# Group sums of a normalisation moved from TensorE to VectorE's shuffles, and one weighted addition of the kernel mixing moved to ScalarE and a DMA

## The chip, the cores and the metric

One core of one Trainium2 chip. The metric is the device time of one execution in microseconds (us), lower is better. TensorE multiplies, VectorE (DVE) and ScalarE (ACT) compute on whole tiles of 128 partitions, GpSimd (POOL) computes little here and issues the accumulating DMAs, SyncE (SP) issues the plain ones.

## The reference

```
x: 16 images, 128 channels, 32 x 32, f32
gn(v): normalise over each group of 4 channels (32 groups), eps 1e-5
routing = sigmoid(mean(gn(x), pixels) @ w_route.T + b_route)   # 4 weights per image
y  = conv3x3(gn(x), w_experts)            # 4 experts, 128 -> 128 channels each
y  = sum over experts of routing[e] * y[e]
h  = x + silu(y * inv + shift)            # inv, shift from the batch-norm parameters
out = h + conv3x3(gn(h), sign(W))
```

The kernel mixes the four experts' weights with an image's routing first, and then does one convolution with the mixed kernel.

## The kernel before

Channels lie on the 128 partitions, so a group of the normalisation is four neighbouring partitions. All 16 images stay in SBUF (tile X, residual added in place). The five engines run five instruction streams that are written out by hand and tied with semaphores. The order of each stream is fixed.

**Image stages.** Image 0 is convolved directly in the head of the program (direct_part), while the weights arrive. Images 1 to 15 use a Winograd-like form along the rows: VectorE makes six points of each 4-row tile (all_rows, inner_rows, transform_minus, transform_plus, transform_ends, into V), TensorE multiplies each point with three taps (minus_points, plus_point, end_points, L562, f32), VectorE brings them back (inverse_sums, inverse_inner, inverse_outer, into y). ScalarE applies SiLU (L936), and POOL adds y to X by an accumulating DMA (residual, L450). That is h. The second convolution, with the sign weights, takes h in two f16 parts: hi and lo (ScalarE's L951 and L958, VectorE's low_part L1309), 18 products each (sign_half, L598).

**The loop.** Iteration t = 1 to 15 of each engine's stream works on several images at once. TensorE does the points of image t and then the sign convolution of image t - 1. VectorE does, in this order, the transforms of image t + 1, its mix with expert 1, the inverse of image t, pool_routes, the low part of image t - 1, the mixes with experts 2 and 3, and the kernel rows (even_rows, kernel_rows) of image t + 1. ScalarE's order in iteration t is quoted below with the statistics.

**The statistics.** The chain of number c normalises two things at once: x of image c (column IN) and h of image c - LAG (column MID), LAG = 3. In iteration t it is c = t + 2. ScalarE fills four columns of stats: the negated means and the sums of squared deviations of both. TensorE multiplies them with a matrix that sums over each group (group_stats, into PSUM tile ps). ScalarE makes variances of it (variances: gdev2, less, two ve), POOL the power -0.5 (power, L446), ScalarE the biases and, from them, hi and hn:

```
var_mid(t - 1); add_variance(c, MID); variances(c)
copy_minus(t); evacuate(t - 2); deviation(c); centring(c); pads(c)
bias(c, MID); split_hi(t - 1); pooled_plane(c); split_hn(t - 1)
silu(t); mean_mid(t); mean_in(c + 1); var_in(c + 1)
squares(c + 1); add_variance(c + 1, IN); routing(c); mix(c)
```

variances(c) waits for the group sums of the column that stands directly before it. In the trace its first instruction is the one that writes gdev (L848). split_hi(t - 1) is what TensorE waits for before its high-part products of iteration t.

**The mixing.** Tile U, three buffers in a ring, holds an image's mixed kernel, 128 x 1152. ScalarE writes route[0] * expert 0 (mix, L908), and VectorE adds the other three in place, one instruction each (mix(i, e), L1186).

**The head.** ScalarE makes the statistics of images 0, 1 and 2 between the four parts of image 0's first mix. The chains of images 1 and 2 go through TensorE (group_mean L510, group_var L521), between the products of image 0 (L552).

Of the kernel before, what the change touches and what calls it, by code (L numbers as in the profile page):

```python
# [10 lines left out]
ALU = mybir.AluOpType  # L11
# [45 lines left out]

RING = 3
QUARTERS = 4

# [7 lines left out]
def build(nc, x, w_experts, w_sign, params, out):  # L68
# [5 lines left out]
    with ExitStack() as ctx:  # L74
# [81 lines left out]
        zr = sb("zr", [C, B])  # L156
        centre = sb("centre", [C, B, 2])
        pooled = sb("pooled", [C, B, E])
        th = sb("th", [C, B, E])
        route = sb("route", [C, B, E])  # L160
# [43 lines left out]
        pooled_ready = sem("pooled_ready")  # L204
        logits_ready = sem("logits_ready")
        th_ready = sem("th_ready")
        route_ready = sem("route_ready")
# [74 lines left out]
        def mixes_before(t):  # L282

            return len(DIRECT_PARTS) * (E - 1) * min(t, ND) + (E - 1) * rank(t)

# [151 lines left out]
        def _(pool):  # L437
# [37 lines left out]
            for t in range(1, B + 1):  # L475
                power(t + LAG - 1)
                if 0 <= t - 2 < B - LATE:
                    add_output(t - 2)
                if ND <= t < B and t not in DVE_RESIDUAL:
                    residual(t)  # L480

        @block.tensor
        def _(pe):
# [38 lines left out]

            def group_stats(c):

                if c < B:
                    pe.wait_ge(nm_in_ready, c + 1)
                pe.wait_ge(nm_mid_ready, c - LAG + 1)
                pe.wait_ge(spread_ready, columns_to(c))
                wait_bank(c)
                step = 1 if c < B else 3  # L530
                mm_(gstats(c, 0, 4, step), gmat[:], stats[:, c, 0:4:step], start=True, stop=True).then_inc(gvar_ready, 1)  # L531

            def route_logits(i):
                pe.wait_ge(pooled_ready, i + 1)
                mm_(logits(i), ones[:], pooled[:, i, :], start=True, stop=True).then_inc(logits_ready, 1)  # L535

# [21 lines left out]

            def point(t, bank, j, k, weights):
                for n, kx in enumerate(KX_ORDER):  # L560
                    c0, c1 = reach(kx, 0, W, W)
                    mm = mm_(bank[:, :, j, c0:c1], tap_weights(weights, kx),  # L562
                             V[t % 2][:, :, k, c0 + kx - 1:c1 + kx - 1], start=(n == 0), stop=(n == K - 1))
                return mm
# [9 lines left out]

            def plus_point(t, j):
                r = rank(t)
                k = (P1, P2)[j]
                pe.wait_ge(v_ready, 5 * r + 4)
                wait(pe, sums_ready, 2 * r)
                pe.wait_ge(kernel_ready, 4 * r + k + 1)  # L580
                mm = point(t, pa, j, k, UM[t % 2][:, k, :])
                if j == 1:
                    mm.then_inc(m_ready, 1)

# [116 lines left out]
            for t in range(1, B + 1):  # L701
                c = t + LAG - 1
                if t < B:
                    minus_points(t)
                    if t > 1:
                        group_stats(c)
                        sign_half(t - 2, 1, 1, TAP_ORDER[-1:])
                    plus_point(t, 0)
                    if t == 1:
                        group_stats(c)  # L710
                    plus_point(t, 1)
                    end_points(t)
                if t == 1:
                    pe.wait_ge(ws_ready, 1)
                if t == B:
                    sign_conv_last()
                elif t == B - 1:
                    sign_half(t - 1, 0, 0)
                    sign_half(t - 1, 0, 1, TAP_ORDER[:5])
                    group_mean(c + 1)  # L720
                    sign_half(t - 1, 0, 1, TAP_ORDER[5:])
                    sign_half(t - 1, 1, 0, TAP_ORDER[:5])
                    last_residual()
                    group_var(c + 1)
                    sign_half(t - 1, 1, 0, TAP_ORDER[5:])
                    sign_half(t - 1, 1, 1)
                else:
                    sign_half(t - 1, 0, 0)
                    sign_half(t - 1, 0, 1)
                    if c < B:  # L730
                        route_logits(c)
                    sign_half(t - 1, 1, 0)
                    sign_half(t - 1, 1, 1, TAP_ORDER[:-1])

        @block.scalar
        def _(act):
# [87 lines left out]
            def deviation(c):  # L824

                if c < B:
                    act.wait_ge(nm_in_ready, c + 1)
                    activation(dev[:, c:c + 1], gnm(c, IN), ACT.Identity, bias=nm(c, IN), scale=-1.0) \
                        .then_inc(dev_ready, 1)
# [6 lines left out]
            def variance(c):  # L836

                k = cols(c)[0]
                last = c == CHAINS - 1
                act.wait_ge(gvar_ready, c + 1)  # L840
                activation(ve[:, c, k:k + 1], gvar(c, k), ACT.Identity, bias=epsilon[:, last:last + 1],
                           scale=1.0 / (HW * (LAST_SCALE if last else ACT_SCALE) ** 2)).then_inc(ve_ready, 1)

            def variances(c):

                a, b = cols(c)
                act.wait_ge(gvar_ready, c + 1)
                activation(gdev2[:, c, a:b], gstats(c, a, b), ACT.Square, bias=base[:, 0:1]).then_inc(gdev2_ready, 1)  # L848
                act.wait_ge(gdev2_ready, c - LAG + 1)
# [3 lines left out]
                for k in range(a, b):  # L853
                    op = activation(ve[:, c, k:k + 1], gvar(c, k), ACT.Identity, bias=less[:, c, k:k + 1],  # L854
                                    scale=1.0 / (HW * ACT_SCALE ** 2))
                op.then_inc(ve_ready, 1)

            def bias(c, k):
                act.wait_ge(rstd_ready, c + 1)
                activation(nbias[:, c, k:k + 1], gnm(c, k), ACT.Copy,  # L860
                           scale=rstd[:, c, k:k + 1]).then_inc((nbias_mid_ready, nbias_in_ready)[k], 1)
# [7 lines left out]
            def centring(i):  # L869

                if in_one(i):
                    act.wait_ge(gvar_ready, i + 1)
                else:
                    act.wait_ge(gnm_ready, gnm_chain(i))
                for n, factor in enumerate((1.0, P1_SUM)):
                    activation(centre[:, i, n:n + 1], gnm(i, IN), ACT.Copy, scale=-factor).then_inc(centre_ready, 1)

# [22 lines left out]
            def mix(i):  # L900
# [176 lines left out]
        def _(dve):  # L1077
# [77 lines left out]
            def top_rows():  # L1155
# [5 lines left out]
                 .then_inc(xn_top_ready, 1)  # L1161

            def pool_routes(c):
                if c < B:
# [285 lines left out]
            for t in range(1, B):  # L1450

                if t == B - 1:
                    sign_points()
                all_rows(t + 1)
                if t == 1:
                    residual(0)
                inner_rows(t + 1)
                transform_minus(t + 1)
                transform_plus(t + 1)
                transform_ends(t + 1)  # L1460
                mix(t + 1, 1)
                inverse_sums(t)
                inverse_inner(t)
# [39 lines left out]
```

## Time and profile before

| | |
|---|---|
| three runs | 273.08, 273.12, 273.42 us, median 273.12 |
| profiled execution | 273.27 us, of which 271.2 us lie between its first and last instruction |
| busy | TensorE 263.0, VectorE 255.0, ScalarE 213.5, POOL 45.2 us |
| granted TensorE clock | 0.999 of full speed, mean |
| DMA | 35.20 MB, 130 GB/s mean |

The profile shows one execution. "Busy" adds up the spans of instructions. The chain that ended last is followed back from the last instruction to what released each step. In a timeline a line gives start, duration, engine, source line, operation, tile written <- tiles read, the count, and in brackets the idle time of that engine before it with what ended it. Consecutive instructions of an engine may overlap by about 0.1 us.

### The profile page before, as it was taken

The numbers are of one execution on the slowest core, as the hardware profiler recorded it, in microseconds if no ns is written. First come the engines' busy times: TensorE is split into PE (matmuls) and PEld (weight loads), VectorE is DVE, ScalarE is ACT, GpSimd is POOL, SyncE is SP. The second block draws the span as 40 slices with busy tenths as digits, with TensorE's granted clock in tenths as the row PEclk, the third lists the DMA queues.
The fourth block names the chain that finished last, engine by engine and source line by source line (L and its number), as shares of the span: only waits on it lengthen the run. The fifth ranks groups of instructions, "written<-read, shape, count | busy, mean of one in ns | idle before, by whom it ended". The sixth has DMA issues, their size and how long they took to land.

```text
span 271.2 us, 4199 instructions
## 1 busy us (share of the span) xinstructions
PE 263.0 (97%) x1339; PEld 182.2 (67%) x1339; DVE 255.0 (94%) x461; ACT 213.5 (79%) x469; POOL 45.2 (17%) x61
## 2 busy tenths in 40 slices
PE   7889899999999999999999999999999999999993
PEld 7545766758485766859586675848576685858663
DVE  5789999999999999999999999999999999995985
ACT  2798898898979788898979799797979886735870
POOL 2011030313121021312112021211202021210110
PEclk9999999999999999999999999999999999999999
DMA  7998856452716455361825546271645536282407
GB/s 205 416 369 300 272 194 155 69 128 51 144 77 111 123 79 155 34 124 77 140 95 77 155 68 148 37 138 80 106 126 79 156 34 124 79 137 97 77 2 155
DMA packets 10245, 35.20 MB, mean 130 GB/s; under 512 B 1264, under 2 KB 1904, under 8 KB 10224
## 3 DMA queue, kind: packets, MB, share of 16 engines
q0 software_dynamic: 4176, 15.21, 33.2%
q1 hardware_dynamic: 5616, 19.34, 19.3%
q10 hardware_dynamic: 432, 0.39, 0.4%
q8 instruction: 11, 0.18, 0.3%
q14 instruction: 10, 0.08, 0.1%
HBM read 11.34 MB, written 16.25 MB: 102 GB/s over the span
## 4 chain that ended last, share of the span: by engine, by line
PE 92%; DMA 3%; DVE 1%; SPq 1%; issue 1%; ACT 0%; DVEq 0%; ACTq 0%
PE pc L598 42%; PE pa L562 14%; PE pe_ L562 14%; PE pb L562 14%; PE pd L552 4%; DMA we<-w_experts 3%; PE ps L531 1%; PE ps L535 1%; SPq L409 0%; PE pa L635 0%; PE pb L635 0%; DVE X L1402 0%; SPq L413 0%; PE pc L521 0%; DVE sums L1384 0%
## 5 line engine op out<-in xcount | busy, mean ns | idle before, releaser
L1186 DVE SCALAR_TENSOR_TENSOR U<-we,route,U 128x1152 f32<-128x1152 f32 x45 | 63.7, 1415 | 0.5
L598 PE MATMUL pc<-lo,ws 128*128 128x496 f16 (+3 forms) x270 | 62.0, 375 | 0.0
L598 PE MATMUL pc<-hi,ws 128*128 128x496 f16 (+3 forms) x270 | 59.8, 375 | 0.0
L598 PEld LDWEIGHTS pc<-hi,ws 128*128 128x128 f16 x270 | 26.4, 98 | 29.3
L598 PEld LDWEIGHTS pc<-lo,ws 128*128 128x128 f16 x270 | 27.7, 106 | 26.3
L446 POOL TENSOR_TENSOR rstd<-ve,nhalf 128x2 f32<-128x2 f32 (+1 forms) x19 | 17.4, 915 | 142.2 <-ACT ve L854 120.5
L562 PE MATMUL pa<-V,UM 128*128 128x256 f32 (+1 forms) x180 | 40.7, 375 | 0.0
L562 PE MATMUL pb<-V,UM 128*128 128x256 f32 (+1 forms) x180 | 40.5, 375 | 0.0
L562 PE MATMUL pe_<-V,U 128*128 128x256 f32 (+1 forms) x180 | 40.5, 375 | 0.0
L562 PEld LDWEIGHTS pb<-V,UM 128*128 128x128 f32 x180 | 34.2, 190 | 5.3 <-issue 0.4
L562 PEld LDWEIGHTS pe_<-V,U 128*128 128x128 f32 x180 | 34.2, 190 | 3.9
L562 PEld LDWEIGHTS pa<-V,UM 128*128 128x128 f32 x180 | 34.0, 190 | 3.5
L936 ACT ACTIVATE y<-y,bn_shift,bn_tiles 128x1024 f32<-128x1024 f32 x14 | 17.4, 1240 | 6.4 <-DVE y L1288 6.4
L450 POOL DMA_DIRECT2D X<-y x14 | 12.4, 882 | 56.6 <-ACT y L936 56.6
L762 ACT ACTIVATE junk_mid<-X,stats 128x1024 f32<-128x1024 f32 x15 | 17.1, 1139 | 5.8 <-DMA X<-y 5.5
L848 ACT ACTIVATE gdev<-ps,base 128x2 f32<-128x2 f32 (+1 forms) x15 | 3.9, 263 | 19.9 <-PE ps L531 19.8
L951 ACT ACTIVATE hi<-X,nbias,rstd 128x1024 f16<-128x1024 f32 (+2 forms) x16 | 18.9, 1187 | 0.5
L908 ACT ACTIVATE U<-we,route 128x1152 f32<-128x1152 f32 x15 | 18.8, 1256 | 0.5
L1309 DVE TENSOR_TENSOR lo<-hn,hi 128x1024 f16<-128x1024 f32 x15 | 18.3, 1219 | 0.4 <-ACT hn L958 0.4
L958 ACT ACTIVATE hn<-X,nbias,rstd 128x1024 f32<-128x1024 f32 x15 | 18.4, 1226 | 0.0
L1218 DVE SCALAR_TENSOR_TENSOR e_rows<-X 128x1024 f32<-128x1024 f32 x15 | 18.3, 1219 | 0.0
L748 ACT ACTIVATE junk_var<-X,stats 128x1024 f32<-128x1024 f32 x15 | 17.2, 1147 | 0.5
(168 smaller groups left out, 400.3 us busy)
## 6 DMA issues: line engine op xcount, KB each, us to landing
X<-x SPq DMA_DIRECT2D x15, 512.0 KB, 5.8
out<-X SPq DMA_DIRECT2D x15, 512.0 KB, 2.6
out<-ev POOLq DMA_DIRECT2D x15, 512.0 KB, 5.5
X<-y POOLq DMA_DIRECT2D x14, 512.0 KB, 4.5
we<-w_experts SPq DMA_DIRECT2D x2, 768.0 KB, 8.8
ws_raw<-w_sign SPq DMA_DIRECT2D x1, 576.0 KB, 11.4
we<-w_experts SPq DMA_DIRECT2D x1, 512.0 KB, 6.6
out<-X SPq DMA_DIRECT2D x1, 384.0 KB, 2.8
```

The lines of the kernel that those rows point to most:

```text
L446: g.tensor_tensor(rstd[:, c, a:b], ve[:, c, a:b], nhalf[:, a:b], ALU.pow).then_inc(rstd_ready, 1)
L562: mm = mm_(bank[:, :, j, c0:c1], tap_weights(weights, kx), V[t % 2][:, :, k, c0 + kx - 1:c1 + kx - 1], start=(n == 0), stop=(n == K - 1))
L598: mm = mm_(rows[:, r0 - first // W:r1 - first // W, c0:c1], ws[:, tap * C:(tap + 1) * C], plane((hi, lo)[part], i)[:, r0 + ky - 1:r1 + ky ...
L748: activation(junk["var"][:], img(i), ACT.Square, bias=nm(i, IN), accum_out=var[:, i, IN:IN + 1]).then_inc(var_in_ready, 1)
L762: activation(junk["mid"][:], img(i), ACT.Square, bias=nm(c, MID), accum_out=var[:, c, MID:MID + 1]).then_inc(var_mid_ready, 1)
L908: activation(nine(U[i % RING]), expert(0), ACT.Copy, scale=route[:, i, 0:1]).then_inc(mix_first, 1)
L936: activation(flat3(y[i % 2][:]), flat3(y[i % 2][:]), ACT.Silu, bias=bn_shift[:, 0:1], scale=bn_tiles[:, 0:1], accum_out=ysum[:, i:i + 1]). ...
L951: activation(plane(hi, i)[:, first:last, :], img(i).rearrange("p (h w) -> p h w", h=H)[:, first:last, :], ACT.Identity, bias=nbias[:, c, M ...
L958: activation(hn[:], img(i), ACT.Identity, bias=nbias[:, c, MID:MID + 1], scale=rstd[:, c, MID:MID + 1]).then_inc(hn_ready, 1)
L1186: v.scalar_tensor_tensor(out=nine(U[i % RING]), in0=expert(e), scalar=route[:, i, e:e + 1], in1=nine(U[i % RING]), op0=ALU.mult, op1=ALU.a ...
L1218: v.scalar_tensor_tensor(out=flat3(e_rows[:]), in0=flat(X[:, i, 0:H, :]), scalar=-4.0, in1=flat(X[:, i, 2:2 + H, :]), op0=ALU.mult, op1=AL ...
L1309: v.tensor_tensor(lo[i % 2][:, 0:HW], hn[:], hi[i % 2][:, 0:HW], ALU.subtract).then_inc(lo_ready, 1)
```

## The change

Three parts, with the order around them:

- **Head.** On ScalarE the deviations and the centring of image 1 stand before the fourth part of the first mix, and variance before pads for images 1 and 2.
- **Group sums.** From chain 3 on, TensorE's group_stats goes. VectorE has group_sums: two rounds of a stream_shuffle within 32 partitions (partition number with bit 1, then bit 2 flipped) and an addition, into gsum. ScalarE reads gsum, and divides by the group size in its scale. It gets one more small activation, middle_mean. group_sums stands behind inner_rows in iterations 2 to 14, behind mix(2, 1) in iteration 1, and first in iteration 15.
- **Mixing.** From image 3 on ScalarE also writes route[1] * expert 1 into a tile (scale_second), and POOL's queue adds this tile to U by an accumulating DMA (add_scaled), behind the residual. VectorE's mix with expert 1 goes for these images. The mixes with experts 2 and 3 stay behind the low part, and the first of them waits for the DMA.

```diff
@@ gpsimd
+            def add_scaled(i):
+                pool.wait_ge(mix_first, firsts_before(i) + 1)
+                pool.wait_ge(scaled_ready, i - SCALED_FROM + 1)
+                g.dma_start(flat(U[i % RING][:]), scaled[:], accum_op=ALU.add).then_inc(scaled_added, 16)
...
                     residual(t)
+                if t + LAG - 1 < B:
+                    add_scaled(t + LAG - 1)
@@ tensor
-            def group_stats(c):
...
-                mm_(gstats(c, 0, 4, step), gmat[:], stats[:, c, 0:4:step], start=True, stop=True).then_inc(gvar_ready, 1)
...
                     minus_points(t)
                     if t > 1:
-                        group_stats(c)
                         sign_half(t - 2, 1, 1, TAP_ORDER[-1:])
-                    plus_point(t, 0)
-                    if t == 1:
-                        group_stats(c)
-                    plus_point(t, 1)
+                    plus_points(t)
                     end_points(t)
@@ scalar
             def variances(c):
...
-                act.wait_ge(gvar_ready, c + 1)
-                activation(gdev2[:, c, a:b], gstats(c, a, b), ACT.Square, bias=base[:, 0:1]).then_inc(gdev2_ready, 1)
+                act.wait_ge(gsum_ready, c - LAG + 1)
+                activation(gdev2[:, c, a:b], gsum[:, c, a:b], ACT.Square, bias=base[:, 0:1],
+                           scale=1.0 / GSIZE).then_inc(gdev2_ready, 1)
...
+            def middle_mean(c):
+                activation(gmid[:, c:c + 1], gsum[:, c, MID:MID + 1], ACT.Copy, scale=1.0 / GSIZE) \
+                    .then_inc(gmid_ready, 1)
...
+            def scale_second(i):
+
+                wait(act, scaled_added, 16 * (i - SCALED_FROM))
+                activation(scaled[:].rearrange("p (g n) -> p g n", n=C), expert(1), ACT.Copy,
+                           scale=route[:, i, 1:2]).then_inc(scaled_ready, 1)
...
             var_in(1)
-            mix_first_part(0, 3)
             deviations(1)
             centring(1)
+            mix_first_part(0, 3)
+            variance(1)
             pads(1)
-            variance(1)
...
             centring(2)
+            variance(2)
             pads(2)
-            variance(2)
...
                 variances(c)
+                middle_mean(c)
...
                     mix(c)
+                    scale_second(c)
@@ vector
+            def group_sums(c):
+
+                a, step = 0, 1 if c < B else 3
+                data = stats[:, c, 0:4:step]
+                if c < B:
+                    dve.wait_ge(nm_in_ready, c + 1)
+                dve.wait_ge(nm_mid_ready, c - LAG + 1)
+                dve.wait_ge(spread_ready, columns_to(c))
+                for n, bit in enumerate((1, 2)):
+                    source = (data, pairs[:, 0:4:step])[n]
+                    target = (pairs[:, 0:4:step], gsum[:, c, 0:4:step])[n]
+                    wait(dve, pairs_ready, c - LAG + n)
+                    v.stream_shuffle(swapped[:, n, 0:4:step], source, [p ^ bit for p in range(32)]) \
+                     .then_inc(swapped_ready, 1)
+                    dve.wait_ge(swapped_ready, 2 * (c - LAG) + n + 1)
+                    op = v.tensor_tensor(target, source, swapped[:, n, 0:4:step], ALU.add)
+                    op.then_inc((pairs_ready, gsum_ready)[n], 1)
...
             def mix(i, e):
...
-                if e == 1:
+                if e < first_mix(i):
+                    return
+                if e > first_mix(i):
+                    dve.wait_ge(mixed, mixes_before(i) + e - first_mix(i))
+                elif e == 1:
                     dve.wait_ge(mix_first, firsts_before(i) + 1)
                 else:
-                    dve.wait_ge(mixed, mixes_before(i) + e - 1)
+                    dve.wait_ge(scaled_added, 16 * (i - SCALED_FROM + 1))
...
             for t in range(1, B):
...
                 if t == B - 1:
+                    group_sums(t + LAG - 1)
                     sign_points()
                 all_rows(t + 1)
                 if t == 1:
                     residual(0)
                 inner_rows(t + 1)
+                if 1 < t < B - 1:
+                    group_sums(t + LAG - 1)
                 transform_minus(t + 1)
                 transform_plus(t + 1)
                 transform_ends(t + 1)
                 mix(t + 1, 1)
+                if t == 1:
+                    group_sums(t + LAG - 1)
                 inverse_sums(t)
```

first_mix(i) is 2 from image SCALED_FROM = 3 on, and 1 before.

## Rows read from the trace of the kernel before

**Rows 1.** The page, busy time and share of the span of each engine.
```profile
...
PE 263.0 (97%) x1339; PEld 182.2 (67%) x1339; DVE 255.0 (94%) x461; ACT 213.5 (79%) x469; POOL 45.2 (17%) x61
...
```

**Rows 2.** The chain that ended last, in order of time: start us, us, what.
```profile
...
36.65 3.81 PE pc L598 x18
...
46.74 0.12 PE ps L531 x2
...
52.16 3.81 PE pc L598 x18
...
222.70 3.81 PE pc L598 x18
...
```

**Rows 3.** Waits from 44.2 to 230 us: us in total, times, longest us.
```profile
...
ACT gdev L848 <- PE ps L531: 16.7, 12, 1.6
...
ACT y L936 <- DVE y L1288: 5.0, 12, 0.7
ACT junk_mid L762 <- DMA X<-y: 1.4, 2, 1.2
...
ACT th L891 <- PE ps L535: 1.1, 1, 1.1
...
```

**Rows 4.** ScalarE: one group of the page, then its timeline in iteration 6.
```profile
...
L908 ACT ACTIVATE U<-we,route 128x1152 f32<-128x1152 f32 x15 | 18.8, 1256 | 0.5
...
108.91 0.26 ACT L848 ACTIVATE gdev<-ps,base 128x2 f32<-128x2 f32 x1 [1.21 <-PE ps L531]
...
112.18 1.24 ACT L951 ACTIVATE hi<-X,nbias,rstd 128x1024 f16<-128x1024 f32 x1
113.33 0.28 ACT L866 ACTIVATE zr<-dev,rstd 128x1 f32<-128x1 f32 x1
113.52 1.23 ACT L958 ACTIVATE hn<-X,nbias,rstd 128x1024 f32<-128x1024 f32 x1
...
```

**Rows 5.** ScalarE's timeline in iteration 1.
```profile
...
32.78 0.26 ACT L848 ACTIVATE gdev<-ps,base 128x2 f32<-128x2 f32 x1
...
33.70 0.26 ACT L828 ACTIVATE dev<-ps,stats 128x1 f32<-128x1 f32 x1
33.85 0.24 ACT L876 ACTIVATE centre<-ps 128x1 f32<-128x1 f32 x2
...
35.34 0.84 ACT L951 ACTIVATE hi<-X,nbias,rstd 128x544 f16<-128x544 f32 x1
...
36.95 1.23 ACT L958 ACTIVATE hn<-X,nbias,rstd 128x1024 f32<-128x1024 f32 x1
38.08 1.23 ACT L936 ACTIVATE y<-y,bn_shift,bn_tiles 128x1024 f32<-128x1024 f32 x1
...
```

**Rows 6.** VectorE's timeline in iterations 1 and 2.
```profile
...
33.04 1.41 DVE L1186 SCALAR_TENSOR_TENSOR U<-we,route,U 128x1152 f32<-128x1152 f32 x1
...
38.21 1.23 DVE L1309 TENSOR_TENSOR lo<-hn,hi 128x1024 f16<-128x1024 f32 x1 [0.42 <-ACT hn L958]
...
46.21 0.68 DVE L1227 TENSOR_TENSOR f_rows<-X 128x512 f32<-128x512 f32 x1
...
```

**Rows 7.** VectorE's timeline, small instructions of the head.
```profile
...
11.77 0.15 DVE L1100 TENSOR_TENSOR bn_full<-bn_rs,prm 128x1 f32<-128x1 f32 x1
11.96 0.16 DVE L1104 TENSOR_TENSOR bn_mscale<-bn_full,prm 128x1 f32<-128x1 f32 x1
12.03 0.15 DVE L1105 TENSOR_SCALAR bn_direct<-bn_full 128x1 f32<-128x1 f32 x1
...
```

**Rows 8.** TensorE's timeline, two stalls of the head.
```profile
...
14.92 0.35 PE L521 MATMUL pc<-stats,gmat 128*128 128x1 f32 x2 [0.73 <-ACT centre L876]
...
32.39 0.36 PE L531 MATMUL ps<-stats,gmat 128*128 128x4 f32 x2 [0.72 <-issue]
...
```

**Rows 9.** The page, DMA issues: KB each, us to landing.
```profile
...
X<-y POOLq DMA_DIRECT2D x14, 512.0 KB, 4.5
...
ws_raw<-w_sign SPq DMA_DIRECT2D x1, 576.0 KB, 11.4
...
```

More of the change, by code:

```diff
@@ L58 @@
 RING = 3
+SCALED_FROM = 3
 QUARTERS = 4
@@ L157, in build @@
         centre = sb("centre", [C, B, 2])
+        scaled = sb("scaled", [C, K * KCO])
         pooled = sb("pooled", [C, B, E])
+        swapped = sb("swapped", [C, 2, 4])
+        pairs = sb("pairs", [C, 4])
+        gsum = sb("gsum", [C, CHAINS, 4])
+        gmid = sb("gmid", [C, CHAINS])
         th = sb("th", [C, B, E])
@@ L205, in build @@
         logits_ready = sem("logits_ready")
+        scaled_ready = sem("scaled_ready")
+        scaled_added = sem("scaled_added")
+        swapped_ready = sem("swapped_ready")
+        pairs_ready = sem("pairs_ready")
+        gsum_ready = sem("gsum_ready")
+        gmid_ready = sem("gmid_ready")
         th_ready = sem("th_ready")
@@ L282, in mixes_before, with first_mix @@
         def mixes_before(t):
-            return len(DIRECT_PARTS) * (E - 1) * min(t, ND) + (E - 1) * rank(t)
+            return len(DIRECT_PARTS) * (E - 1) * min(t, ND) + sum(E - first_mix(i) for i in range(ND, t))
+        def first_mix(i):
+            return 2 if i >= SCALED_FROM else 1
         def firsts_before(t):
@@ L521, in group_var @@
                 mm_(gvar(c, k), gmat[:], data, start=True, stop=True).then_inc(gvar_ready, 1)
[L523 to L531 removed]
             def route_logits(i):
                 pe.wait_ge(pooled_ready, i + 1)
+                if i > LAG:
+                    pe.wait_ge(th_ready, i)
                 mm_(logits(i), ones[:], pooled[:, i, :], start=True, stop=True).then_inc(logits_ready, 1)
@@ L557, in direct_part, with point @@
                     mm.then_inc(direct_ready, 1)
-            def point(t, bank, j, k, weights):
-                for n, kx in enumerate(KX_ORDER):
+            def point(t, bank, j, k, weights, taps=KX_ORDER):
+                for kx in taps:
                     c0, c1 = reach(kx, 0, W, W)
                     mm = mm_(bank[:, :, j, c0:c1], tap_weights(weights, kx),
-                             V[t % 2][:, :, k, c0 + kx - 1:c1 + kx - 1], start=(n == 0), stop=(n == K - 1))
+                             V[t % 2][:, :, k, c0 + kx - 1:c1 + kx - 1], start=(kx == KX_ORDER[0]),
+                             stop=(kx == KX_ORDER[-1]))
                 return mm
@@ L827, in deviation @@
                     act.wait_ge(nm_in_ready, c + 1)
-                    activation(dev[:, c:c + 1], gnm(c, IN), ACT.Identity, bias=nm(c, IN), scale=-1.0) \
+                    mean, scale = (gsum[:, c, IN:IN + 1], -1.0 / GSIZE) if in_one(c) else (gnm(c, IN), -1.0)
+                    activation(dev[:, c:c + 1], mean, ACT.Identity, bias=nm(c, IN), scale=scale) \
                         .then_inc(dev_ready, 1)
@@ L839, in variance @@
                 last = c == CHAINS - 1
-                act.wait_ge(gvar_ready, c + 1)
+                act.wait_ge(gvar_ready, LAG + 1 if last else c + 1)
                 activation(ve[:, c, k:k + 1], gvar(c, k), ACT.Identity, bias=epsilon[:, last:last + 1],
@@ L853, in variances @@
                 for k in range(a, b):
-                    op = activation(ve[:, c, k:k + 1], gvar(c, k), ACT.Identity, bias=less[:, c, k:k + 1],
-                                    scale=1.0 / (HW * ACT_SCALE ** 2))
+                    op = activation(ve[:, c, k:k + 1], gsum[:, c, 3 - k:4 - k], ACT.Identity,
+                                    bias=less[:, c, k:k + 1], scale=1.0 / (GSIZE * HW * ACT_SCALE ** 2))
                 op.then_inc(ve_ready, 1)
+            def middle_mean(c):
+                activation(gmid[:, c:c + 1], gsum[:, c, MID:MID + 1], ACT.Copy, scale=1.0 / GSIZE) \
+                    .then_inc(gmid_ready, 1)
             def bias(c, k):
                 act.wait_ge(rstd_ready, c + 1)
-                activation(nbias[:, c, k:k + 1], gnm(c, k), ACT.Copy,
+                if in_one(c):
+                    act.wait_ge(gmid_ready, c - LAG + 1)
+                activation(nbias[:, c, k:k + 1], gmid[:, c:c + 1] if in_one(c) else gnm(c, k), ACT.Copy,
                            scale=rstd[:, c, k:k + 1]).then_inc((nbias_mid_ready, nbias_in_ready)[k], 1)
@@ L871, in centring @@
                 if in_one(i):
-                    act.wait_ge(gvar_ready, i + 1)
+                    act.wait_ge(gsum_ready, i - LAG + 1)
+                    mean, share = gsum[:, i, IN:IN + 1], 1.0 / GSIZE
                 else:
                     act.wait_ge(gnm_ready, gnm_chain(i))
+                    mean, share = gnm(i, IN), 1.0
                 for n, factor in enumerate((1.0, P1_SUM)):
-                    activation(centre[:, i, n:n + 1], gnm(i, IN), ACT.Copy, scale=-factor).then_inc(centre_ready, 1)
+                    activation(centre[:, i, n:n + 1], mean, ACT.Copy, scale=-factor * share).then_inc(centre_ready, 1)
             def pads(i):
```

12 lines of the change are left out of this document (5 added, 7 removed).

## The prediction, made before the change was run

> **What bounds the kernel now.** I read the page first: TensorE is busy for 97% of the span [rows 1]. Then the chain of waits, in order of time: from 36.65 us on it is TensorE's products almost alone, one image after the other. Call H(t) the start of the high-part products in iteration t. H(1) is 36.65, H(2) 52.16, H(13) 222.70, so one iteration takes (222.70 - 52.16)/11 = 15.50 us [rows 2]. The group products, which the change takes off TensorE, are 0.12 us of it.
>
> The waits between 44.2 and 230 us (12 iterations) show the room of the others [rows 3]. ScalarE waits 16.7 + 5.0 + 1.4 + 1.1 = 24.2 us, 2.0 per iteration, so its own work, start to start, is 15.50 - 2.0 = 13.5 us. The reader should see what most of this room is: 1.4 us per iteration in which ScalarE has delivered its last column and needs the group sums back (gdev behind ps). It is a round trip through another engine, and there is no work of ScalarE's order between its two ends. It can get shorter, not vanish.
>
> **What the change removes.** TensorE loses 14 group products of 0.12 us (t = 2 to 15) and, in iteration 1, one of 0.36 with a stall of 0.72 before it [rows 2, 8]. Its own iteration becomes 15.38. VectorE loses one mix of 1.41 us in the iterations that mix images 3 to 15. VectorE is not what ends last, so this pays only by letting something else start sooner.
>
> **What it adds on ScalarE.** Three things, in each of iterations 2 to 13. First scale_second: 128x1152, the shape of the first mix, 1.26 us [rows 4], less 0.10 that two long activations overlap (36.95 + 1.23 against 38.08, [rows 5]): 1.16. Second middle_mean, a one-column activation from SBUF. One such starts 0.19 after the last (113.33 to 113.52, [rows 4]): 0.19. Third, five small activations (two ve, dev, two centre) now read gsum in SBUF instead of PSUM. With a PSUM source the next starts 0.15 later (33.70 to 33.85, [rows 5]), with an SBUF source 0.19. I take 0.05 each, and 0.02 for gdev2: 0.27. The lower end of the last two items is 0.15 together (no difference by source). Sum 1.16 + 0.46 = 1.62.
>
> **The round trip through VectorE.** It has four instructions, each waiting for the one before: shuffle, add, shuffle, add. Two dependent small adds start 0.19 apart (11.77 to 11.96), undependent ones 0.07 (11.96 to 12.03) [rows 7]. No row shows a shuffle; I price it as an add, because the tile has only four columns. That gives 4 x 0.19 = 0.76, and 0.07 for the two handoffs between engines (hn ends at 36.95 + 1.23 = 38.18, lo starts at 38.21, [rows 5, 6]): 0.83. Ends: 4 x 0.07 + 0.07 = 0.35; and ScalarE's dependent small steps, of which 32.78 to 33.70 holds two beside two of 0.15 [rows 5], so 0.31 each: 4 x 0.31 + 0.07 = 1.31.
>
> **The sum for one iteration.** ScalarE: 13.5 + 1.62 + 0.83 = 15.95 us. That is more than TensorE's 15.38, and more than the 15.50 of now. TensorE then waits 0.57 us per iteration for hi. A second loop says nearly the same without the price of scale_second. From S, the start of gdev, ScalarE reaches the start of hn after 4.61 us (108.91 to 113.52) and its end 1.23 later; with 0.46 of additions this is S + 6.3. VectorE's low part waits for hn. From low part to the end of the inner rows, where group_sums stands, VectorE needs 46.21 - 38.21 + 0.68 = 8.7 us, with two mixes in it as after the change [rows 6]. With the handoffs and the four instructions that is 6.3 + 8.7 + 0.83 = 15.8. So the mix that is taken from VectorE frees nothing at this place. It was the third one, in front of the inverse sums, and there VectorE will stand and wait for TensorE.
>
> The Trainium skill, "Vector Engine (DVE) Microarchitecture Reference", section "The reshape front-end and per-opcode configuration", says that a shuffle uses lane selectors that an instruction of its own has loaded before. No row here shows one. The two masks differ, so by that rule each group_sums would hold two more instructions on the round trip.
>
> **The DMA.** add_scaled is one transfer of 576 KB on POOL's queue. X<-y, 512 KB between the same memories, lands 4.5 us after issue [rows 9]; by size 5.1. ws_raw, 576 KB in the crowded head, took 11.4: the upper end. VectorE wants it at its next low part plus 1.2. From the end of scale_second that is 1.6 (var_mid and its column, estimated as hn's 1.23 and two small steps) + 0.83 + 6.3 + 1.2 = 9.9 us. So it is hidden with 4.8 us to spare. If it took 11.4, each image would wait 1.5. POOL's issue is a part of those 4.5 us. It stands in front of power(t + 3), whose input comes 1.6 + 0.83 and three small steps after scale_second, over 3 us: hidden too. The DMA of the residual is issued and landed before add_scaled is issued.
>
> **The head.** TensorE's stall of 0.73 before group_var(1) [rows 8] ends sooner. The next column (image 2) then sets the limit, so I take 0.45 of the 0.73; ends 0 and 0.73. But in iteration 1 group_sums(3) is put behind mix(2, 1), which starts at 33.04 and takes 1.41 [rows 6]. VectorE is running, so only the handoff back is added to its 0.76. So S(1) = 33.04 - 0.45 + 1.41 + 0.80 = 34.80, where it was 32.78 [rows 5]. The first part of hi ended 35.34 + 0.84 - 32.78 = 3.40 after S, through POOL's power; with 0.10 for the dearer ve, H(1) = 38.30 instead of 36.65. TensorE, whose other work is now done at 36.65 - 0.45 - 0.72 - 0.36 = 35.1, idles some 3 us there. silu(1) started 38.08 - 32.78 = 5.30 after S, so now at 34.80 + 5.30 + 0.12 = 40.22. S to silu is 4.61 + 1.13 + 0.46 = 6.20 of the loop of 15.95, so S(2) = 40.22 + 9.75 = 49.97. hi ends 112.18 + 1.24 - 108.91 = 4.51 after S [rows 4]; with 0.46 and 0.05 for the handoff, H(2) = 54.99, which is 2.83 late.
>
> **The end.** H(2) to H(13) is 11 loops of 15.95 instead of 15.50: +4.9, so H(13) is 7.7 late. From iteration 13 on ScalarE has no next image to take statistics of (two activations over 1024 columns are gone, each about the 1.23 of hn), so TensorE is the bound again and saves 0.12 twice: +7.5. The profiled execution took 273.27: 280.8. The runs' median is 0.15 below it: 280.6.
>
> **The rivals.**
> A (0.52): ScalarE's loop binds as worked out, 277.5 to 284. Its lower end has the small activations at 0.15 together: a loop of 15.64, some 12 x 0.31 = 3.7 less.
> B (0.20): each shuffle brings a further instruction on the round trip. At 0.07 each, 13 round trips (the first and iterations 2 to 13) cost 0.14 x 13 = 1.8 more: 282.4. At 0.19 it is 4.9 more, 285.5. This is the rule cited above.
> C (0.08): the chain of four runs at its lower end, 0.35. The loop is 15.47, TensorE's nearly, and the late H(2) remains: 2.83 - 2 x 0.48 - 11 x 0.03 - 0.24 = +1.3, 274.4 for the median, and up to 277 between here and A.
> D (0.07, the other side): TensorE stays the bound and sheds its products. It is decided at a loop of 15.38 on both ScalarE and VectorE, so additions plus round trip under 1.9 us instead of 2.45. With H(1) at its best, 33.04 - 0.73 + 1.41 + 0.32 + 3.40 = 37.44 (+0.8), and 14 x 0.12 saved: -0.9, 272.4. For it speaks that ScalarE waits 2.0 now, against it that 1.4 of this is a round trip that stays. Between C and D lies no change to be measured (0.03), about 273.1.
> E (0.05): the idle 3 us before H(1) lower TensorE's clock. The granted clock is full throughout this trace, with the longest pause since the start 0.73. If the first 3.8 us of products [rows 2] took twice as long, TensorE would reach H(2) at 38.30 + 15.38 + 3.8 = 57.5 instead of 54.99: 283.1. "TensorE: Matmul & The Clock Gate" of the Trainium skill, Part 1, states that an idle TensorE falls back to half its clock; no run here shows it yet.
> F (0.05): the scaled expert lands late, 11.4 us after issue. Then 1.5 per loop on VectorE's side, of which 0.2 is room: some +14, over 290.
>
> **The numbers.** Faster 0.07, within 0.2% (what this kernel's runs can tell) 0.03, slower 0.90. From 276.5 to 285.0 leaves out D, the middle case, part of C, F and the far part of B, together under 0.2.
>
> **What the profile after would show.** Right: in iterations 2 to 13 gdev waits for VectorE's gsum (0.8 to 1.0 us) and no longer for ps. ScalarE waits for nothing else. H(t) is 15.9 to 16.0 apart up to t = 13, then 15.4. TensorE shows a pause of about 3 us before H(1) and 0.5 before each further one, ended by hi. VectorE waits before sums for pa and before lo for hn. mix(i, 2) never waits for the DMA. Wrong: H(t) 15.4 apart (D), an idle VectorE before U ended by a DMA (F), a granted clock under 1 around 38 us (E), or group_sums over 1.0 us from first to last (B). The weakest numbers are the price of a shuffle, as it enters 13 times, and the place of S(1).

## The result, and the profile after

The changed kernel takes 281.04 us (median of four runs, 280.57 to 281.40) against 273.10 us (272.78 to 273.42). The ratio is 1.029, with a 95% interval of 1.027 to 1.031: slower. The forecast was 280.6.

The page of the changed kernel: busy time of the engines, the shares of the chain that ended last, the group of the ScalarE instruction that waits for the sums, and the new DMA.

```profile
span 279.6 us, 4252 instructions
...
PE 264.7 (95%) x1309; PEld 178.8 (64%) x1309; DVE 248.4 (89%) x538; ACT 231.0 (83%) x497; POOL 53.9 (19%) x74
...
ACT 43%; PE 21%; issue 18%; DVE 13%; DMA 1%; POOL 1%; DVEq 0%; ACTq 0%; SPq 0%
...
L860 ACT ACTIVATE gdev<-gsum,base 128x2 f32<-128x2 f32 (+1 forms) x15 | 4.4, 296 | 16.9 <-DVE gsum L1207 16.9
...
U<-scaled POOLq DMA_DIRECT2D x13, 576.0 KB, 5.1
```

TensorE led the chain before. Its shares then, from the page of the kernel before:

```profile
PE 92%; DMA 3%; DVE 1%; SPq 1%; issue 1%; ACT 0%; DVEq 0%; ACTq 0%
```

Now ScalarE has 43% of it and TensorE 21%, although TensorE still has the largest busy share. A busy share alone would not have shown this.

Its waits between 50 and 230 us (total, times, longest):

```profile
...
ACT gdev L860 <- DVE gsum L1207: 12.2, 12, 1.0
...
DVE lo L1360 <- ACT hn L985: 7.3, 10, 0.7
PE pc L613 <- ACT hi L978: 4.3, 10, 0.4
DVE swapped L1204 <- ACT stats L832: 3.5, 11, 0.4
DVE sums L1313 <- PE pa L577: 1.1, 1, 1.1
ACT y L963 <- DVE y L1339: 0.3, 1, 0.3
```

Of ScalarE's 2.0 us of waits per iteration [rows 3] one is left, 1.0 us, for gsum. TensorE waits for hi, VectorE for hn and for ScalarE's column: all three wait for ScalarE.

TensorE's timeline, the starts of the high-part products, H(1), H(2), H(3), H(12), H(13) and H(14):

```profile
38.04 5.65 PE L613 MATMUL pc<-hi,ws 128*128 128x512 f16 x18 [3.09 <-ACT hi L978]
...
55.09 3.97 PE L613 MATMUL pc<-hi,ws 128*128 128x512 f16 x18
...
70.97 1.23 PE L613 MATMUL pc<-hi,ws 128*128 128x512 f16 x5 [0.36 <-ACT hi L978]
...
214.80 3.98 PE L613 MATMUL pc<-hi,ws 128*128 128x512 f16 x18 [0.44 <-ACT hi L978]
...
230.78 3.98 PE L613 MATMUL pc<-hi,ws 128*128 128x512 f16 x18 [0.44 <-ACT hi L978]
...
246.16 3.97 PE L613 MATMUL pc<-hi,ws 128*128 128x512 f16 x18
```

From H(3) to H(13) it is (230.78 - 70.97)/10 = 15.98 us per iteration, then 15.38 once ScalarE has no more image to prepare. Timelines show these starts 0.16 to 0.17 us earlier than the chain of waits of [rows 2]. Both are read alike in all the kernels below: by timelines, the kernel before has H(1) 36.49, H(2) 51.99, H(13) 222.53 and H(15) 253.40.

ScalarE's timeline around the round trip of iteration 2, and VectorE's in the same stretch:

```profile
45.95 1.24 ACT L935 ACTIVATE scaled<-we,route 128x1152 f32<-128x1152 f32 x1
47.09 1.14 ACT L773 ACTIVATE junk_mid<-X,stats 128x1024 f32<-128x1024 f32 x1
...
48.41 0.29 ACT L832 ACTIVATE stats<-dev,var 128x1 f32<-128x1 f32 x1
49.73 0.30 ACT L860 ACTIVATE gdev<-gsum,base 128x2 f32<-128x2 f32 x1 [1.02 <-DVE gsum L1207]
...
54.65 1.23 ACT L985 ACTIVATE hn<-X,nbias,rstd 128x1024 f32<-128x1024 f32 x1
```

```profile
48.92 0.01 DVE L1204 LOAD_MASK_SELECT swapped<-stats  x1 [0.31 <-ACT stats L832]
48.94 0.16 DVE L1204 STREAM_SHUFFLE swapped<-stats 128x4 f32<-128x4 f32 x1
49.13 0.16 DVE L1207 TENSOR_TENSOR pairs<-stats,swapped 128x4 f32<-128x4 f32 x1
49.34 0.01 DVE L1204 LOAD_MASK_SELECT swapped<-pairs  x1
49.34 0.15 DVE L1204 STREAM_SHUFFLE swapped<-pairs 128x4 f32<-128x4 f32 x1
49.53 0.16 DVE L1207 TENSOR_TENSOR gsum<-pairs,swapped 128x4 f32<-128x4 f32 x1
```

The column ends at 48.70 and ScalarE goes on at 49.73. In between it does nothing, and VectorE does four instructions of 0.16 us. Each starts 0.19 to 0.21 after the one it waits for.

### The profile page after: what moved, and what is told of

Its sections match the earlier page's. It is cut to its first block, busy times and chain, and to the rows that moved or that the text cites. A ratio compares the mean times of both kernels' runs of the same rounds, so it can differ in the third digit from the quotient of the medians.

```text
span 279.6 us, 4252 instructions
## 1 busy us (share of the span) xinstructions
PE 264.7 (95%) x1309; PEld 178.8 (64%) x1309; DVE 248.4 (89%) x538; ACT 231.0 (83%) x497; POOL 53.9 (19%) x74
## 4 chain that ended last, share of the span: by engine, by line
ACT 43%; PE 21%; issue 18%; DVE 13%; DMA 1%; POOL 1%; DVEq 0%; ACTq 0%; SPq 0%
PE pc L613 12%; ACT y L963 5%; ACT scaled L935 5%; ACT junk_mean L753 4%; ACT junk_mid L773 4%; ACT hn L985 4%; ACT ev L1017 4%; PE pa L577 3%; PE pb L577 3%; DVE U L1237 2%; ACT minus L952 2%; PE pe_ L577 2%; ACT route L918 2%; DVE swapped L1204 1%; ACT stats L832 1%
## 5 line engine op out<-in xcount | busy, mean ns | idle before, releaser
L613 PE MATMUL pc<-hi,ws 128*128 128x496 f16 (+3 forms) x270 | 61.6, 383 | 7.9 <-ACT hi L978 7.9
L1237 DVE SCALAR_TENSOR_TENSOR U<-we,route,U 128x1152 f32<-128x1152 f32 x32 | 45.3, 1416 | 0.5
L613 PEld LDWEIGHTS pc<-lo,ws 128*128 128x128 f16 x270 | 26.5, 102 | 26.6
L462 POOL TENSOR_TENSOR rstd<-ve,nhalf 128x2 f32<-128x2 f32 (+1 forms) x19 | 14.6, 770 | 73.2 <-ACT ve L867 51.7
L471 POOL DMA_DIRECT2D U<-scaled x13 | 11.3, 873 | 69.5 <-ACT scaled L935 69.5
L773 ACT ACTIVATE junk_mid<-X,stats 128x1024 f32<-128x1024 f32 x15 | 17.1, 1137 | 5.0 <-DMA X<-y 4.7
L860 ACT ACTIVATE gdev<-gsum,base 128x2 f32<-128x2 f32 (+1 forms) x15 | 4.4, 296 | 16.9 <-DVE gsum L1207 16.9
```

The source lines that it names most:

```text
L462: g.tensor_tensor(rstd[:, c, a:b], ve[:, c, a:b], nhalf[:, a:b], ALU.pow).then_inc(rstd_ready, 1)
L613: mm = mm_(rows[:, r0 - first // W:r1 - first // W, c0:c1], ws[:, tap * C:(tap + 1) * C], plane((hi, lo)[part], i)[:, r0 + ky - 1:r1 + ky ...
L773: activation(junk["mid"][:], img(i), ACT.Square, bias=nm(c, MID), accum_out=var[:, c, MID:MID + 1]).then_inc(var_mid_ready, 1)
```

## The experiments

H values are TensorE's timeline starts of the high-part products, as above. "Per iteration" is their distance in the steady part.

**The head alone.** The kernel before, with deviations(1) and centring(1) ahead of the first mix's fourth part and variance ahead of pads:

```diff
-            mix_first_part(0, 3)
             deviations(1)
             centring(1)
-            pads(1)
-            variance(1)
+            mix_first_part(0, 3)
+            variance(1)
+            pads(1)
```

> The kernel before with the head's reordering alone. My theory (TensorE's stall of 0.73 us before the group product of image 1 ends, image 2's column then limits): 0.45 us less, 272.6 to 272.7, the stall under 0.1. Rival (the head has slack that eats it): no change, 273.1.

Measured 272.66 against 273.04, ratio 0.998 (0.9966 to 0.9995). H(1) is 36.06, 0.43 sooner, and every later H keeps the 0.43. This part of the change is a gain, carried to the end. The stall before group_var(1) is gone:

```profile
13.41 1.08 PE L552 MATMUL pd<-xn,U 128*128 128x496 f32 x2
14.44 0.35 PE L521 MATMUL pc<-stats,gmat 128*128 128x1 f32 x2
14.66 1.91 PE L552 MATMUL pd<-xn,U 128*128 128x496 f32 x4
```

In the kernel before, that product started at 14.92 with 0.73 of idle time ahead of it [rows 8].

**The group sums without the scaled expert.** SCALED_FROM = 16 in the changed kernel, so VectorE mixes three experts for every image:

```diff
-SCALED_FROM = 3
+SCALED_FROM = 16
```

> The changed kernel without the scaled expert: VectorE mixes experts 1, 2 and 3 as before, group sums stay on VectorE. My theory (two loops): ScalarE's loop falls to 15.98 - 1.14 = 14.8 us, but VectorE's own work of 15.26 plus the 0.7 of group_sums makes 15.9 to 16.0 us per iteration, now VectorE-bound: 280 to 281.5. Rival (only ScalarE's copy made the kernel slower): TensorE bound at 15.38, 274 to 275.

Measured 280.70, ratio 1.027 (1.024 to 1.030), 15.92 per iteration. The window of one iteration (stretch, its length, busy time and instructions of TensorE, weight loads, VectorE, ScalarE, POOL, granted clock, DMA) shows which engine is full:

```profile
118.88:134.80 15.92, 15.54 (x74) 10.50 (x75) 15.74 (x33) 13.53 (x31) 2.50 (x3) 1.00 0.48 100
```

VectorE is busy for 15.74 of 15.92, and the trace has no wait of VectorE for another engine in this stretch. This is as expected. So group sums on VectorE by themselves cost 0.4 us per iteration: VectorE has to lose a mix to carry them. The two parts of the change need each other, and the kernel with both is no faster than this one.

**The scaled expert without the group sums.** The kernel before, with scale_second, add_scaled and mix(i, e) from the change, group_stats left on TensorE:

```diff
                     mix(c)
+                    scale_second(c)
...
+                if t + LAG - 1 < B:
+                    add_scaled(t + LAG - 1)
```

> The kernel before with the scaled expert alone: group sums stay on TensorE, the head as before. My theory (ScalarE's loop is its work plus the round trip): 13.5 + 1.16 + about 0.6 for the shortest round trip through TensorE = 15.3, just under TensorE's 15.50, so 15.5 per iteration and 273.1 to 273.9. Rival (the copy and the DMA cost by themselves, in contention or on POOL's queue): 0.3 us or more in each of 12 iterations, over 276.

Measured 275.94, ratio 1.010 (1.007 to 1.013), 15.68 per iteration. Both theories missed: 0.18 per iteration more than TensorE's own 15.50, and not 0.3. H(2), at 52.93, is 0.94 late besides (iteration 1 has a copy too). The two together make the 2.9 us by which H(15) is late (256.30 against 253.40). The timelines of TensorE, then ScalarE, then VectorE in iteration 3 show what I had left out:

```profile
60.48 2.70 PE L577 MATMUL pb<-V,UM 128*128 128x256 f32 x12
63.12 0.36 PE L546 MATMUL ps<-stats,gmat 128*128 128x4 f32 x2
...
63.53 2.70 PE L577 MATMUL pa<-V,UM 128*128 128x256 f32 x12
```

```profile
62.62 0.29 ACT L836 ACTIVATE stats<-dev,var 128x1 f32<-128x1 f32 x1
63.51 0.26 ACT L863 ACTIVATE gdev<-ps,base 128x2 f32<-128x2 f32 x1 [0.60 <-PE ps L546]
...
69.67 1.24 ACT L957 ACTIVATE y<-y,bn_shift,bn_tiles 128x1024 f32<-128x1024 f32 x1 [0.32 <-DVE y L1314]
```

```profile
66.34 0.69 DVE L1288 TENSOR_TENSOR sums<-pa,minus 128x512 f32<-128x512 f32 x1 [1.66 <-PE pa L577]
```

The group product waits for ScalarE's column (ended at 62.91, product at 63.12) and holds the plus points that are queued behind it. They hold VectorE's inverse, this holds silu, and silu holds the next column. From 63.12 it is 3.22 us to VectorE's sums, 3.33 to silu at 69.67, 8.92 to the end of the next column and 0.21 to the next product: 15.68. This is a loop over y. ScalarE's own loop would be this minus the 0.32 it waits for y, 15.36, near the 15.3 expected. So the copy on ScalarE costs by its length, as worked out, and 0.32 comes through a queue. The steps of this loop leave no place for a DMA or for POOL, so the rival's cause, contention or POOL's queue, does not show.

**group_sums(3) earlier.** In iteration 1 of the changed kernel:

```diff
                 transform_plus(t + 1)
+                if t == 1:
+                    group_sums(t + LAG - 1)
                 transform_ends(t + 1)
                 mix(t + 1, 1)
-                if t == 1:
-                    group_sums(t + LAG - 1)
```

> The changed kernel with group_sums(3) of iteration 1 moved from behind mix(2, 1) to between the points P2 and the end points of image 2, 2 us earlier. My theory (the place in iteration 1 delays everything behind it, and the pause of 3.1 us brings TensorE's clock down): H(1) at 36 instead of 38.04, the granted clock full at 39 to 43 us, H(2) at 52.7 instead of 55.09, then 15.98 per iteration as before: 278.6 to 279.0. Rival (the delay of iteration 1 is absorbed by the ScalarE loop, which sets H(2) anyway): 281.0.

Measured 279.82 (279.33 to 281.68), ratio 1.026 (1.021 to 1.031). H(1) is 36.55, H(2) 53.12, H(13) 228.86 instead of 230.78, and 15.98 per iteration is unchanged. The gain in the profiles is 1.9 us, the 1.9 by which the four instructions moved. The medians differ by 1.2, with four executions that spread over 2.35 us, and 279.82 lies between the expected 278.6 to 279.0 and the rival's 281.0. The delay in iteration 1 is not absorbed. I had expected 2.4 at H(2), and it is 1.97.

**No copy on ScalarE.** The changed kernel scales expert 1 for image 3 only, and the DMA adds that tile for all images. Left out are 12 scalings, so the mixed kernels of images 4 to 15 are not the reference's:

```diff
                     mix(c)
-                    scale_second(c)
+                    if c == SCALED_FROM:
+                        scale_second(c)
...
-                pool.wait_ge(scaled_ready, i - SCALED_FROM + 1)
+                pool.wait_ge(scaled_ready, 1)
+                if i > SCALED_FROM:
+                    pool.wait_ge(mixed, mixes_before(i - 1) + 1)
```

> The changed kernel in which ScalarE scales expert 1 once, for image 3, and the DMA adds that same tile for all images 3 to 15; 12 scale_second are left out, so the mixed kernels of images 4 to 15 are not the reference's. ScalarE's loop falls to 15.98 - 1.14 = 14.84. My theory (a second loop from hn over low part, two mixes, kernel rows, rows and group_sums back to gdev, which in the changed kernel has only the 0.32 us to spare that VectorE waits for the column): 15.66 per iteration, 277.4 to 277.8. Rival (ScalarE's loop alone): TensorE bound, 15.38, 274.5.

Measured 276.74, ratio 1.015 (1.012 to 1.018), 15.57 per iteration. Taking 1.14 us off ScalarE gave back 0.41. ScalarE now waits 17.1 us for gsum in ten waits between 70 and 230 us, 1.7 each. The loop over hn and VectorE exists. I had put it at 15.66 from a wait of 0.32, and it is 15.57; the time is below the expected 277.4 too.

**Work inside the round trip.** mean_in of the next image between the column and variances, on ScalarE, in iterations 2 and later:

```diff
                     add_variance(c, MID)
+                    if c + 1 < B:
+                        mean_in(c + 1)
                 variances(c)
...
-                if c + 1 < B:
+                if c + 1 < B and t == 1:
                     mean_in(c + 1)
```

> The changed kernel with mean_in of the next image (1.14 us, needs nothing of this iteration) moved on ScalarE between the last column and variances, so that work stands inside the round trip. ScalarE's own loop falls by the 1.0 us of the wait to 15.0. My theory: VectorE's loop of 15.66 binds, gdev still waits some 0.7 us for gsum although there is work in between: 277.4 to 277.8. Rival (the round trip was hidden and that was all): 15.38, 274.5. If the wait comes back elsewhere (the residual's DMA, 6.1 us after silu starts, against 6.2 that are left in front of var_mid): up to 0.3 more.

Measured 276.59, ratio 1.013 (1.012 to 1.015), 15.56 per iteration: the same bound as without the copy, and again below the expected 277.4 to 277.8. ScalarE's timeline, and VectorE's in the same stretch:

```profile
101.57 1.23 ACT L985 ACTIVATE hn<-X,nbias,rstd 128x1024 f32<-128x1024 f32 x1
...
110.34 1.04 ACT L753 ACTIVATE junk_mean<-X 128x1024 f32<-128x1024 f32 x1
...
112.22 0.30 ACT L860 ACTIVATE gdev<-gsum,base 128x2 f32<-128x2 f32 x1 [0.75 <-DVE gsum L1209]
...
117.14 1.23 ACT L985 ACTIVATE hn<-X,nbias,rstd 128x1024 f32<-128x1024 f32 x1
```

```profile
102.83 1.23 DVE L1362 TENSOR_TENSOR lo<-hn,hi 128x1024 f16<-128x1024 f32 x1 [0.33 <-ACT hn L985]
...
112.02 0.16 DVE L1209 TENSOR_TENSOR gsum<-pairs,swapped 128x4 f32<-128x4 f32 x1
```

The wait of 1.0 has work in it now, and 0.75 of waiting is left, because VectorE comes to group_sums later than the column. The lines close the loop: from hn to the low part 1.26, from there to gsum 9.19 in which VectorE waits for nothing, 0.20 to gdev, and 4.92 to the next hn, together 15.57. Two quite different edits of ScalarE end at the same 15.56 to 15.57.

**group_sums first.** As the last, and in VectorE's order group_sums before all_rows instead of behind inner_rows:

```diff
+                if 1 < t < B - 1:
+                    group_sums(t + LAG - 1)
                 all_rows(t + 1)
...
                 inner_rows(t + 1)
-                if 1 < t < B - 1:
-                    group_sums(t + LAG - 1)
```

> As the one with mean_in moved, and group_sums on VectorE moved from behind inner_rows to before all_rows, 1.74 us earlier in its order (iterations 2 to 14). My theory: both loops are now under 15.38, TensorE is the bound again from H(2) on: 55.1 + 13 x 15.38, so 274.3 to 274.9. Rival (the loop is not what limits, but the sum of ScalarE's work and its DMA waits): 15.6 or more, 277.

Measured 279.22, ratio 1.022 (1.020 to 1.024), 15.71 per iteration, dearer than my theory and than the rival's 277. The theory as I wrote it was wrong. VectorE now waits for the column with the whole of the rows and transforms queued behind, and ScalarE waits for y:

```profile
112.27 0.01 DVE L1206 LOAD_MASK_SELECT swapped<-stats  x1 [1.00 <-ACT stats L832]
```

```profile
104.32 1.24 ACT L963 ACTIVATE y<-y,bn_shift,bn_tiles 128x1024 f32<-128x1024 f32 x1 [0.80 <-DVE y L1341]
```

It is the loop over y again, through VectorE's queue this time instead of TensorE's. Followed back from one silu (120.04) to the one before (104.32), the chain holds only ScalarE's work up to the column and VectorE's from the sums to y, 15.72 us with no work of TensorE in it.

**The same with two more edits.** group_sums(3) earlier as above, and the scaled expert from image 4 on.

```diff
-SCALED_FROM = 3
+SCALED_FROM = 4
```

> As the last, and group_sums(3) two us earlier in iteration 1, and the scaled expert only from image 4 on, so that iteration 1 has no scale_second. My theory: H(1) at 36.5, S(2) at 47.25, H(2) at 52.3 instead of 55.1, then 15.38 per iteration: H(15) 1.3 us before that of the kernel before, 271.6 to 272.2, faster than the kernel before by 0.4%. Rival (a third of a us is lost somewhere in each iteration, as the rooms are under 0.3 us everywhere): 274 or more.

Measured 277.72, ratio 1.017 (1.016 to 1.020), again 15.71 per iteration. I had expected 271.6 to 272.2. It is in the rival's range (274 or more), with its reason now known: the same loop over y. H(1) and H(2) came as expected (36.46 and 52.02), but H(3) is 17.05 later. In iteration 2 VectorE waits 1.04 for the column and does the third mix as well, and TensorE waits 0.58 for lo and 0.62 for UM.

**group_sums between all_rows and inner_rows.** With mean_in in the round trip and group_sums(3) early:

```diff
                 all_rows(t + 1)
...
+                if 1 < t < B - 1:
+                    group_sums(t + LAG - 1)
                 inner_rows(t + 1)
-                if 1 < t < B - 1:
-                    group_sums(t + LAG - 1)
```

> The changed kernel with mean_in inside the round trip, group_sums(3) early in iteration 1, and group_sums of iterations 2 to 14 between all_rows and inner_rows. Behind inner_rows the loop over hn took 15.56 us, in front of all_rows VectorE stood 1.0 us for the column and the loop over y took 15.71. Between the two the first falls by 0.60 to 14.96 and the second by the wait of 1.0 to 14.7. My theory (the longest of four loops counts): TensorE's 15.38 from H(2) = 53.1 on, H(15) 0.5 us before that of the kernel before: 272.4 to 272.8. Rival (a further loop of 15.5 or more that I don't see, as before): 274 or more.

Measured 272.67 against 273.15, ratio 0.998 (0.997 to 0.999), 15.37 per iteration, H(2) 53.11, H(15) 252.75. Here no loop is longer than TensorE's own work. Its waits between 70 and 230 us:

```profile
DVE sums L1315 <- PE pa L577: 6.5, 10, 0.7
ACT y L963 <- DVE y L1341: 4.2, 11, 0.4
ACT th L912 <- PE ps L550: 1.1, 1, 1.1
ACT gdev L860 <- DVE gsum L1209: 1.0, 1, 1.0
```

VectorE waits for TensorE again, and gdev waits once instead of in each iteration. Each iteration is 0.13 shorter than in the kernel before. That H(2) comes 1.12 later takes most of this back.

**The same, scaled from image 4 on.** Again with SCALED_FROM = 4, as in the kernel with the two more edits.

> As the one with group_sums between all_rows and inner_rows, and the scaled expert only from image 4 on: iteration 1 loses scale_second (1.14 us on ScalarE), iteration 2 gets a mix of 1.34 us more on VectorE, in front of the inverse sums. My theory: S(2) 1.1 us earlier, but y of image 2 0.8 us after hn, so that H(3) is only 0.3 us earlier than in the sibling: 272.1 to 272.6. Rival (the saved 1.1 us stays): 271.5.

Measured 272.46, ratio 0.9975 (0.996 to 0.999). H(2) is 52.19, H(3) 68.12 against 68.48 in its sibling, H(15) 252.39. The 0.9 won at H(2) is lost to 0.36 at H(3), as worked out. It is the best version measured, and the difference to its sibling is within the spread of both. Neither is told apart from the head's edit alone (0.998).

**The pause filled.** The changed kernel, with 52 unused products where TensorE pauses before H(1):

```diff
                 if t == 1:
                     pe.wait_ge(ws_ready, 1)
+                    pe.wait_ge(silu_ready, 1)
+                    warm(52)
```

> The changed kernel in which TensorE fills the pause before H(1) with 52 unused 128x128 products (about 2.8 us at full speed, ended before hi is there). In the changed kernel's profile the granted clock is 0.59 from 39 to 43 us and the first 18 products take 5.65 us; in two other kernels with the same pause it stayed full, and H(2) - H(1) was 16.57 instead of 17.05. My theory (the pause costs by ScalarE's lateness, the clock adds a little, and not in every execution): the clock full, H(2) 0.5 us earlier, the median 0.2 to 0.5 us under the changed kernel's 281.0. Rival (the half clock is what makes iteration 1 dear): over 1.5 us faster.

Measured 281.01 (280.72 to 281.57), ratio 1.029 (1.027 to 1.030). The windows (length, TensorE busy, granted clock, DMA) before and in the first products, of the changed kernel (with all engines, as above) and then of this one (TensorE alone):

```profile
35.00:39.00 4.00, 0.96 (x5) 0.53 (x6) 3.01 (x9) 3.79 (x13) 0.84 (x1) 0.99 0.39 160
39.00:43.00 4.00, 4.00 (x13) 1.48 (x12) 3.06 (x4) 3.94 (x7) 1.05 (x1) 0.59 0.02 4
```

```profile
35.00:39.00 4.00, 3.89 (x58) 1.00 0.46 180
39.00:43.00 4.00, 4.00 (x22) 1.00 0.00 0
```

The clock stayed full, H(2) is 54.72 instead of 55.09, and the median did not move, where I had expected 0.2 to 0.5 us. So the rival is out: the lost time of iteration 1 is ScalarE's lateness. What the half clock adds, 0.4 us at H(2) and 0.3 from H(3) to the end in this pair of profiles, is not resolved in the medians. The four executions of the changed kernel fit a small cost: mean granted clocks of 0.991 and 0.990 go with 281.40 and 281.20 us, 0.999 twice with 280.57 and 280.89. Only the first of them has a profile, so where the clock fell in the others is not shown.

## Why the prediction was right

The forecast (280.6, range 276.5 to 285.0, slower) came out within 0.5 us of the median, and by its own steps: A, ScalarE's loop, binds. Part of the closeness is luck, as two sizes were off and cancel.

- **The round trip decides.** Predicted 0.83, measured 1.02. The four instructions took 0.77 (48.92 to 49.69), against the 0.76 taken. The handoff from ScalarE to VectorE was mis-sized: 0.22 instead of 0.03. I had read it off hn to lo. So C, whose chain of four took 0.35 with its handoffs, did not come.
- **Additions on ScalarE.** scale_second 1.14 from start to start (predicted 1.16). From gdev to hn it is 54.65 - 49.73 = 4.92 against 4.61 before, so middle_mean and the SBUF sources are 0.31, not 0.46. With the round trip: 13.5 + 1.14 + 0.31 + 1.02 = 15.97. The two errors cancel by luck: 15.95 was predicted, 15.98 measured.
- **The second loop.** Predicted 15.8, and that it would hold without scale_second. It holds, at 15.56 to 15.57 in two experiments, so it was some 0.25 too long in the forecast. I had also said that VectorE would wait for pa before the inverse sums. It does so once, in iteration 2. In the others it waits 0.7 for hn and 0.3 for the column.
- **The head.** With S as in the prediction, the start of gdev: S(1) predicted 34.80, measured 34.63; S(2) 49.97 and 49.73. H(1) predicted 38.30, by timeline 38.04; H(2) 54.99, by timeline 55.09. In this profile H(2) was set by TensorE, with most of its first 18 products at half clock, and not by hi: VectorE waits 1.13 us for pa there. With the pause filled and the clock full, hi set it, at 54.72. That 54.99 and 55.09 are so close is luck.
- **The end.** H(13) is 8.25 late (predicted 7.7), half of the difference from H(2) and half from the eleven iterations. The whole span is 8.4 longer, the medians differ by 7.9 (predicted 7.5).
- **The rivals.** B's instruction exists. By the rule of the Trainium skill cited beside it ("Vector Engine (DVE) Microarchitecture Reference", section "The reshape front-end and per-opcode configuration") a shuffle uses selectors that an instruction of its own has loaded, and the trace agrees: a LOAD_MASK_SELECT stands before each of the two shuffles. But it lasts 0.01 us, not 0.07 or more, so A and B differ by next to nothing. E's mechanism was there: after 3.09 us of idling the granted clock is 0.59 between 39 and 43 us. This is the rule of the Trainium skill cited beside E, and the trace agrees with it in direction. The size was off twice. From 39 to 42 us the granted clock was 0.50, the 1.2 GHz level, and it was full again before the next products, so that the 18 products took 5.65 instead of 3.97: 1.7 us lost, where E had 3.8. And hi, not TensorE, has the say in the following iterations, which eats most of such a delay. D (TensorE stays the bound) would have been right with three further edits in the two orders. F did not come: U<-scaled landed 5.1 us after issue, as estimated.
- **Two slips in the working.** 3.7 less than 280.6 is 276.9, not A's lower end of 277.5. D's 272.4 starts from the profiled execution; from the median it is 272.2. Neither changes the forecast.
- **What I missed.** The loop over y. At the place where the change put group_sums it was not the longest, so the forecast did not suffer. My later expectations for the scaled expert alone, for group_sums first and for the same with two more edits did.

Where the expected gain went: TensorE's 0.12 per iteration and VectorE's mix were both real. They were off the loop that the change made the longest, which is all of ScalarE's work of one iteration, the copy included, and the round trip for the group sums, in which it has nothing to do.

## What to carry to other kernels

When several engines are nearly full in a hand-ordered loop, add up closed loops, not engines: an engine's own work plus every round trip in which it has nothing to do. Moving a small operation to a less busy engine pays only if its position in that engine's queue is right: in front of too much it makes others wait (15.71), behind too much it comes late (15.56), and here the place between the two gave 15.37, TensorE's own work. Even so no version was told apart from the one with the head's edit alone: a late start in iteration 1 took back what the shorter iterations gave. Put independent work between sending a value out and needing it back before anything is moved for a small gain in throughput.

## What the runs showed that I had not expected

- The clock did not fall every time. With a pause of about 3 us at the same place, the granted clock stayed full in the profiles of the kernels without the copy and with group_sums first, and H(2) - H(1) was 16.57 there. In three others it was 0.57 to 0.59 in the mean from 39 to 43 us, and the difference was 17.04 or 17.05. In the changed kernel it fell only after the products had begun again at 38.04: it is 0.93 from 38.20 to 39.00, 0.50 from 39 to 42 and 0.85 from 42 to 43. Why it fell in some and not in others was not tried.
- POOL's power of the same 128x2 tile had a median of 0.72 us in the changed kernel and 1.92 us in the one with group_sums between the row steps. It cost nothing there in the steady part, since ScalarE's bias, which needs it, starts 2.1 us behind ve. But it ends only 0.12 us before the bias starts, so a slower one would be on ScalarE's loop. What sets it was not tried.
